# Rotary attention of a two-layer decoder: scores of two slots by 64-row strips, the maximum taken off by VectorE, one exponential to a slot

## The chip, the cores and the metric

The kernel runs on one core of one Trainium2 chip. The metric is the device time of one execution in microseconds (us). All data are float32. The engines are named as in the profile: PE is TensorE, DVE VectorE, ACT ScalarE, POOL GpSimd, SP SyncE.

## The reference, cut to what matters

A post-norm decoder of two layers works on 64 sequences of 128 tokens and 128 features. In each layer stand self attention, cross attention against a context of 77 positions, and a mixture of eight experts, each followed by a layer norm of `x + f(x)`. The change concerns the cross attention of the second layer alone, the "rotary" one:

```
q = rms_norm(heads(x @ Wq.T), q_norm_w)         # 16 heads of 8
k = rms_norm(heads(context @ Wk.T), k_norm_w)
v = heads(context @ Wv.T)
q, k = apply_rope(q, q_cos, q_sin), apply_rope(k, k_cos, k_sin)
attn = softmax(einsum('bhtd,bhsd->bhts', q, k) * 8 ** -0.5)
x = layernorm(x + einsum('bhts,bhsd->bhtd', attn, v) @ Wo.T)
```

## The kernel before

The program is six stages one behind the other: "taylor", "wide", "gelu", "causal", "rotary", "swiglu". Three of them ("wide", "causal", "rotary") are built by one function, `softmax_attention`, with `kind` choosing between variants. There is no scheduler: each engine has its instructions in the order in which the function `step` of that engine writes them, and engines meet at semaphores.

The work of the rotary stage is a pipeline over 32 pairs of sequences. A pair has `NU` = 8 **slots**; a slot is four heads (`HU`) of one sequence, so its scores are 128 queries by 4 x 77 keys. In one step an engine runs over the eight slots k = 0 to 7 and does at each what is due for pairs at different depths of the pipeline: `e` and `roots` (norm and rotation of a coming pair), `f` (turning queries and keys), `c` (scores of the current pair), `u` (its output), and behind these the layer norm and the choice of experts ("route") of older pairs.

For the current pair a slot goes like this. POOL makes `keys` of the slot (`make_keys`, L616): the transposed keys, repeated for four heads and multiplied by a mask that leaves each head its 8 rows of 128. PE multiplies the queries `qT` (128 rows, all 16 heads) with them into one of two PSUM banks `s_bank` (L982). DVE takes the negated maximum of each head (L1400). ACT does four exponentials, one to a head, out of the bank with that maximum as bias (L1116). PE transposes them (L991, two slots later), ACT copies them (L1103), and PE multiplies them with the values (L1014, three slots later); a column of ones among the values gives the softmax sum. The bank is free again when the exponentials have read it (`exps_done`).

Four uses share one further bank, `f_bank`, in this order within a pair: PE turns x and projects queries and keys of a coming pair (L728 at slot 0, L752/L753 at slot 1), and DVE reads the products with the rotation tables (L1452 at slot 2, L1454 and L1455 at slot 3); PE turns back the output sums of the first sequence (L911, slot 4) and DVE divides them (L1363, L1367, slot 4, waiting for `back_ps`); PE turns rotated queries and keys (L760, slot 5), for which it waits for that division (`norm_done`); the same division for the second sequence at slot 6, and the values (L756) at slot 7, which waits for it again. L925 turns the divided output, L930 projects it, L880 and L886 serve the choice of experts, and L1187 to L1195 are steps of an inverse root by Newton's method (12 to two pairs, one at slots 0 to 3 of every pair and at slots 4 to 7 of every second).

The causal stage has done since before what the change brings here: masks for eight heads (`heads8`), two matmuls of 64 rows each (L968), and DVE as the first reader of both banks (`add_slopes`, L1358).

Of the kernel before, what the change touches and what calls it, by code (L numbers as in the profile page):

```python
# [22 lines left out]
P = 128  # L23
# [370 lines left out]
def softmax_attention(chip, kind, n_seq, X, ctxT_dram, w, consts, route=None, fill=None, opening=None, later_loads=()):  # L394
# [5 lines left out]
    H = 16  # L400
# [19 lines left out]
    ES = 4 if kind == "causal" else 3 if late else SLOTS  # L420
    BS = 4
    KH = 8 if kind == "causal" else H
    with ExitStack() as ctx:
# [11 lines left out]
        keys = sb("keys", [P, 2, H, 2, NK] if kind == "wide" else [P, 2, KH, NK])  # L435
# [41 lines left out]
        if kind == "causal":  # L477
            biased = sb("biased", [P, BS, HU * NK])
            heads8 = sb("heads8", [P, KH])
            value_row = sb("value_row", [P, NC, P])  # L480
            q_bias = sb("q_bias", [P, 1])
# [43 lines left out]
        PREPARED = {"wide": 3, "causal": 4, "rotary": 10}[kind]  # L525
# [18 lines left out]
        POOL_KEYS = (0, 1)  # L544
# [3 lines left out]
        def first_head(j):  # L548

            return 8 * (j % 2) + 4 * (j // 2) if kind == "causal" else HU * j  # L550
# [57 lines left out]
        def make_keys(engine, pair, piece):  # L608

            engine.wait_ge(front_done, pair.count(FU, 1 if kind == "rotary" else 2))  # L610
            if pair.back(1).real:
                engine.wait_ge(s_ps, pair.back(1).count(NU, 2 * piece + 2 if kind == "causal" else piece + 1))
            b, j = divmod(piece, KH // HU)
            heads = slice(HU * j, HU * (j + 1))
            mask = heads8[:] if kind == "causal" else consts["heads16"]
            engine.tensor_tensor(keys[:, b, heads], kT[:, pair.c % 2, b, 0:NK].unsqueeze(1).to_broadcast([P, HU, NK]),  # L616
                                 mask[:, heads].unsqueeze(2).to_broadcast([P, HU, NK]),
                                 ALU.mult).then_inc(keys_done[piece % 2], 1)

        def keys_ahead(engine, f, c, k, pieces):  # L620

            pair, piece = (f, k - NU + KEYS_LEAD) if k >= NU - KEYS_LEAD else (c, k + KEYS_LEAD)
            if kind == "causal":
                if pair is not None and piece % 2 == 0:
                    make_keys(engine, pair, piece // 2)
            elif pair is not None and piece % 2 in pieces:
                make_keys(engine, pair, piece)

        @block.gpsimd
        def _(pool):  # L630
# [34 lines left out]
            def step(e, roots, f, c, u, n, r=None, *later):  # L665
                for k in range(NU):
                    if sending(later, k) is not None:
                        scatter(*sending(later, k))
                    if kind != "wide":
                        keys_ahead(pool, f, c, k, POOL_KEYS)  # L670
# [145 lines left out]
        def _(pe):  # L816
# [131 lines left out]
            def step(e, roots, f, c, u, mine=None, r=None, q=None, ranked=None, *later):  # L948
                for k in range(NU):
# [6 lines left out]
                    if c is not None:  # L956
# [3 lines left out]
                        if kind == "causal":  # L960
                            if k % 2 == 0:
                                pe.wait_ge(keys_done[k // 2 % 2], c.count(2, k // 4 + 1))
                                if before(c, k, 1) is not None:
                                    bc, bk = before(c, k, 1)
                                    pe.wait_ge(biased_done, bc.count(NU, bk + 1))
# [1143 lines left out]
```

## Time and profile before

| | |
|---|---|
| median of 3 runs | 3026.99 us (3024.47 to 3029.35) |
| profiled execution, its own time | 3017.08 us |
| its span | 3015.3 us |
| PE busy over the span | 2737.1 us (91%) |
| ACT | 2070.9 us (69%) |
| PEld (weight loads) | 1982.6 us (66%) |
| DVE | 1805.1 us (60%) |
| POOL | 1460.1 us (48%) |
| rotary scores on PE, 256 slots | 2061 us to 2600 us of the span |

### The profile page before, as it was taken

The page shows a single profiled execution, that of the slowest core. Times are in us where ns is not written, and L with a number is a line of the kernel's source. Part 1 is how long each engine was busy: PE and PEld are TensorE (multiplying, and loading weights), DVE is VectorE, ACT ScalarE, POOL GpSimd, SP SyncE. Part 2 cuts the span into 40 slices and gives each one's busy share as a digit, 9 for nine tenths or more (in the row PEclk, how much of TensorE's full clock was granted, in tenths as well). Part 3 has the DMA queues.
Part 4 walks back from the last instruction along what each step waited for, and adds up shares of the span by engine and source line. Part 5 has one row for each costly group of instructions (what it writes and reads, how often), then busy time and mean ns, then how long its engine had stood idle before and what let it go on. Part 6 is the DMA issues. An engine that isn't in the chain of part 4 may idle for free. (4 is left out here: it accounts for less than half of the span.)

```text
span 3015.3 us, 69304 instructions
## 1 busy us (share of the span) xinstructions
PE 2737.1 (91%) x21504; PEld 1982.6 (66%) x21504; DVE 1805.1 (60%) x5293; ACT 2070.9 (69%) x7235; POOL 1460.1 (48%) x1978
## 2 busy tenths in 40 slices
PE   8999999999999956998799999978999999699987
PEld 6666777777777746998355555546776666458874
DVE  6883344443444444554688888876677776444545
ACT  6766778777787743443699999976888888522224
POOL 3442224444444454555433333325678887724665
PEclk9999999999999987999899999998999999799998
DMA  9910030220400402221310000000000010001225
GB/s 264 338 47 15 19 116 16 80 78 20 129 27 20 135 30 72 73 70 57 115 56 10 9 10 8 10 22 10 13 27 28 29 31 17 29 26 56 80 79 185
DMA packets 179960, 185.08 MB, mean 61 GB/s; under 512 B 32844, under 2 KB 168537, under 8 KB 179216
## 3 DMA queue, kind: packets, MB, share of 16 engines
q1 hardware_dynamic: 162032, 145.14, 16.1%
q0 software_dynamic: 17280, 34.13, 3.4%
q8 instruction: 181, 2.97, 0.4%
q14 instruction: 179, 1.47, 0.2%
q10 hardware_dynamic: 288, 1.38, 0.2%
HBM read 58.34 MB, written 111.48 MB: 56 GB/s over the span
## 5 line engine op out<-in xcount | busy, mean ns | idle before, releaser
L678 POOL TENSOR_TENSOR wide_probs<-wide_exps,wide_inv_sum 128x308 f32<-128x308 f32 x256 | 179.3, 700 | 488.9 <-DVE wide_inv_sum L1409 486.0
L1400 DVE TENSOR_REDUCE wide_neg_max<-banks 128x4 f32<-128x308 f32 x256 | 122.5, 478 | 473.6 <-PE banks L982 448.9
L1116 ACT ACTIVATE causal_exps<-causal_biased,causal_neg_max 128x128 f32<-128x128 f32 x1024 | 325.8, 391 | 31.1 <-DVE causal_neg_max L1400 29.7
L1119 ACT ACTIVATE wide_exps<-banks,wide_neg_max 128x77 f32<-128x77 f32 x1024 | 315.8, 326 | 0.3 <-DVE wide_neg_max L1400 0.2
L658 POOL DMA_INDIRECT sorted_x<-send,place_i x240 | 244.9, 1020 | 96.0 <-issue 40.5
L1116 ACT ACTIVATE rotary_exps<-banks,rotary_neg_max 128x77 f32<-128x77 f32 x1024 | 252.0, 351 | 15.1 <-DVE rotary_neg_max L1400 13.7
L1103 ACT ACTIVATE wide_probsT<-banks 77x512 f32<-77x512 f32 x256 | 152.1, 594 | 153.6 <-PE banks L991 149.5
L1656 ACT ACTIVATE gelu_hidden<-banks,gelu_slot 128x256 f32<-128x256 f32 x284 | 116.7, 471 | 157.3 <-PE banks L1833 153.1
L1587 POOL DMA_INDIRECT results<-swiglu_tile_out,swiglu_dest_i x142 | 147.7, 1040 | 141.2 <-DVE swiglu_tile_out L1738 97.8
L1119 ACT ACTIVATION_READ_ACCUMULATOR wide_exps<-banks,wide_neg_max 128x1 f32 x1024 | 213.9, 209 | 0.0
L1587 POOL DMA_INDIRECT results<-gelu_tile_out,gelu_dest_i x142 | 140.8, 991 | 142.3 <-DVE gelu_tile_out L1743 119.0
L1358 DVE TENSOR_TENSOR causal_biased<-banks,regions 128x512 f32<-128x512 f32 x256 | 164.6, 685 | 72.3 <-PE banks L968 69.9
L1400 DVE TENSOR_REDUCE rotary_neg_max<-banks 128x4 f32<-128x308 f32 x256 | 121.5, 475 | 120.8 <-PE banks L982 116.4
L982 PE MATMUL banks<-wide_keys,wide_xT 128*128 128x308 f32 x512 | 191.8, 455 | 1.9 <-ACT wide_xT L769 1.6
L982 PE MATMUL banks<-rotary_keys,rotary_qT 128*128 128x308 f32 x512 | 189.0, 451 | 3.5 <-ACT rotary_exps L1116 3.4
L616 POOL TENSOR_TENSOR rotary_keys<-rotary_kT,rest 128x308 f32<-128x308 f32 x256 | 177.4, 708 | 20.0 <-ACT rotary_kT L803 16.5
L991 PEld LDWEIGHTS banks<-first,causal_exps 128*128 128x128 f32 x1024 | 108.9, 141 | 116.3 <-ACT causal_exps L1116 61.0
L1103 ACT ACTIVATE rotary_probsT<-banks 77x512 f32<-77x512 f32 x256 | 157.7, 616 | 34.7 <-PE banks L991 34.1
L735 PE MATMUL banks<-wide_ctxT,wide_product 128*128 128x154 f32 x1024 | 169.9, 299 | 3.3 <-ACT wide_product L1038 0.7
L1400 DVE TENSOR_REDUCE causal_neg_max<-causal_biased 128x4 f32<-128x512 f32 x256 | 169.6, 673 | 0.5 <-ACT causal_exps L1116 0.4
L991 PE MATMUL banks<-first,causal_exps 128*128 128x128 f32 x1024 | 166.1, 285 | 3.1 <-ACT causal_exps L1116 3.0
L1014 PE MATMUL banks<-wide_probsT,wide_values 77*64 77x128 f32 x2048 | 168.3, 285 | 0.1
(382 smaller groups left out, 7339.3 us busy)
## 6 DMA issues: line engine op xcount, KB each, us to landing
sorted_x<-blank SPq DMA_DIRECT2D x1, 34848.0 KB, 116.8
sorted_x<-blank SPq DMA_DIRECT2D x4, 8712.0 KB, 30.3
gelu_tile_in<-sorted_x SPq DMA_DIRECT2D x71, 132.0 KB
swiglu_tile_in<-sorted_x SPq DMA_DIRECT2D x71, 132.0 KB
gelu_back<-results SPq DMA_DIRECT2D x16, 512.0 KB, 7.7
swiglu_back<-results SPq DMA_DIRECT2D x16, 512.0 KB, 6.2
X<-in_x SPq DMA_DIRECT2D x8, 512.0 KB, 7.3
regions<-in_g_w SPq DMA_DIRECT2D x2, 2048.0 KB, 20.9
```

Source lines behind the costliest of these rows:

```text
L616: engine.tensor_tensor(keys[:, b, heads], kT[:, pair.c % 2, b, 0:NK].unsqueeze(1).to_broadcast([P, HU, NK]), mask[:, heads].unsqueeze(2).t ...
L658: pool.indirect_dma_start(route["sorted_x"], bass.IndirectOffsetOnAxis(ap=r_place_i[:, b % 2, which, n // 2:n // 2 + 1], axis=0), send[:, ...
L678: pool.tensor_tensor(probs[:, m % SLOTS], exps[:, m % SLOTS], inv_sum[:, m % SLOTS].unsqueeze(2).to_broadcast([P, HU, NK]), ALU.mult).then ...
L735: last = pe.matmul(f_bank[:, n * 2 * NK:(n + 1) * 2 * NK], product[:, first + n], ctxT[:, s4, :, 0:NK], start=True, stop=True)
L982: pe.matmul(s_bank[k % 2][:, 0:HU * NK], q, moving, start=True, stop=True).then_inc(s_ps, 1)
L991: last = pe.transpose(p_bank[n % 2][0:NK, h * P:(h + 1) * P], exps[:, (NU * pair.c + n) % ES, h] if late else probs[:, n % SLOTS, h], ident)
L1014: last = pe.matmul(o_bank[g % 2][row:row + STRIP, col:col + P], values[0:NK, pair.c % 2, b, first_head(j) + h], probsT[0:NK, n % 2, h * P: ...
L1103: act.activation(probsT[0:NK, n % 2], p_bank[n % 2][0:NK], ACT.Copy).then_inc(probsT_done, 1)
L1116: last = act.activation(exps[:, (NU * c.c + k) % ES, h], scores[:, h * NK:(h + 1) * NK], ACT.Exp, bias=neg_max[:, k % SLOTS, h:h + 1])
L1119: last = act.activation(exps[:, k % SLOTS, h], scores[:, h * NK:(h + 1) * NK], ACT.Exp, bias=neg_max[:, k % SLOTS, h:h + 1], accum_out=exp ...
L1400: dve.tensor_reduce(neg_max[:, k % SLOTS], scores.rearrange("p (h n) -> p h n", h=HU), AX.X, ALU.max, negate=True).then_inc(max_done, 1)
L1587: pool.indirect_dma_start(results, bass.IndirectOffsetOnAxis(ap=dest_i[:, t % YR, j:j + 1], axis=0), tile_out[:, t % YR, j], None, bounds_ ...
```

## The change

1. Keys are masked for eight heads instead of sixteen (`KH` = 8, `heads8`, one added DVE instruction in the stage's opening), so one POOL instruction serves two slots; queries and keys keep their 128 rows.
2. At every even slot PE does the scores of two slots as two matmuls of 64 rows: rows 0 to 63 (heads 0 to 7) into one bank, rows 64 to 127 (heads 8 to 15) into the other. The order of heads over slots changes with it (`first_head`).
3. At every even slot DVE takes the maxima of both slots (`find_top`) and then subtracts them, reading the banks and writing to SBUF (`take_top`, into `biased`). PE may use the banks again after that (`biased_done`), no longer after the exponentials.
4. ACT does one exponential of 308 columns to a slot, from `biased`, in place of four of 77. `exps` has four buffers instead of three.

```diff
-    ES = 4 if kind == "causal" else 3 if late else SLOTS
+    ES = 4 if late else SLOTS
-    KH = 8 if kind == "causal" else H
+    KH = 8 if late else H
...
-                engine.wait_ge(s_ps, pair.back(1).count(NU, 2 * piece + 2 if kind == "causal" else piece + 1))
+                engine.wait_ge(s_ps, pair.back(1).count(NU, 2 * piece + 2))
...
+                        if late and k % 2 == 0:
+                            pe.wait_ge(keys_done[k // 2 % 2], c.count(2, k // 4 + 1))
+                            if before(c, k, 1) is not None:
+                                bc, bk = before(c, k, 1)
+                                pe.wait_ge(biased_done, bc.count(NU, bk + 1))
+                            for n in range(2):
+                                rows = slice(64 * n, 64 * n + 64)
+                                pe.matmul(s_bank[n][:, 0:HU * NK], qT[rows, c.c % 2, b], keys[rows, b, HU * (j // 2):HU * (j // 2) + HU],
+                                          start=True, stop=True).then_inc(s_ps, 1)
...
-                        act.wait_ge(max_done, c.count(NU, k + 1))
-                        scores = biased[:, k % BS] if kind == "causal" else s_bank[k % 2]
+                        act.wait_ge(biased_done if kind == "rotary" else max_done, c.count(NU, k + 1))
+                        scores = biased[:, k % BS] if late else s_bank[k % 2]
...
+                        if kind == "rotary":
+                            last = act.activation(exps[:, (NU * c.c + k) % ES].rearrange("p h n -> p (h n)"), scores, ACT.Exp)
...
+                dve.tensor_tensor(heads8[:], consts["heads16"][:, 0:KH], consts["heads16"][:, KH:2 * KH], ALU.add).then_inc(prepared, 1)
...
+            def find_top(c, k):
+                dve.wait_ge(s_ps, c.count(NU, k + 1))
+                if before(c, k, SLOTS) is not None:
+                    bc, bk = before(c, k, SLOTS)
+                    dve.wait_ge(biased_done, bc.count(NU, bk + 1))
+                dve.tensor_reduce(neg_max[:, k % SLOTS], s_bank[k % 2][:, 0:HU * NK].rearrange("p (h n) -> p h n", h=HU), AX.X,
+                                  ALU.max).then_inc(max_done, 1)
+
+            def take_top(c, k):
+                dve.wait_ge(max_done, c.count(NU, k + 1))
+                if before(c, k, BS) is not None:
+                    bc, bk = before(c, k, BS)
+                    dve.wait_ge(exps_done, bc.count(NU, bk + 1))
+                dve.tensor_tensor(biased[:, k % BS].rearrange("p (h n) -> p h n", h=HU),
+                                  s_bank[k % 2][:, 0:HU * NK].rearrange("p (h n) -> p h n", h=HU),
+                                  neg_max[:, k % SLOTS].unsqueeze(2).to_broadcast([P, HU, NK]), ALU.subtract).then_inc(biased_done, 1)
...
+                    if c is not None and kind == "rotary" and k % 2 == 0:
+                        find_top(c, k)
+                        find_top(c, k + 1)
+                        take_top(c, k)
+                        take_top(c, k + 1)
```

How the order on two engines changes is seen in one pair. The first place is DVE in the fifth pair, from slot 2 to the first division at slot 4. Before:

```order
L1400 TENSOR_REDUCE rotary_neg_max<-banks 128x4
L1444 TENSOR_REDUCE rotary_qk_sum<-rotary_qk_sq 128x64
L1452 TENSOR_TENSOR rotary_turned<-banks,rotary_tables 128x512
L1193 SCALAR_TENSOR_TENSOR rotary_root_part<-rotary_root_part,rotary_qk_sum 128x128
L1400 TENSOR_REDUCE rotary_neg_max<-banks 128x4
L1454 TENSOR_TENSOR rotary_crossed<-banks,rotary_tables 128x64x4
L1455 TENSOR_TENSOR rotary_crossed<-banks,rotary_tables 128x64x4
L1195 SCALAR_TENSOR_TENSOR rotary_qk_rstd<-rotary_root_part,rotary_qk_rstd 128x128
L1400 TENSOR_REDUCE rotary_neg_max<-banks 128x4
L1363 RECIPROCAL rotary_inv_total<-banks 128x16
L1367 TENSOR_TENSOR rotary_o<-banks,rotary_inv_total 128x128
```

And changed, the same stretch (L1357 is `find_top`, L1365 `take_top`, L1372 and L1376 the division):

```order
L1357 TENSOR_REDUCE rotary_neg_max<-banks 128x4 x2
L1365 TENSOR_TENSOR rotary_biased<-banks,rotary_neg_max 128x308 x2
L1458 TENSOR_REDUCE rotary_qk_sum<-rotary_qk_sq 128x64
L1466 TENSOR_TENSOR rotary_turned<-banks,rotary_tables 128x512
L1185 SCALAR_TENSOR_TENSOR rotary_root_part<-rotary_root_part,rotary_qk_sum 128x128
L1468 TENSOR_TENSOR rotary_crossed<-banks,rotary_tables 128x64x4
L1469 TENSOR_TENSOR rotary_crossed<-banks,rotary_tables 128x64x4
L1187 SCALAR_TENSOR_TENSOR rotary_qk_rstd<-rotary_root_part,rotary_qk_rstd 128x128
L1357 TENSOR_REDUCE rotary_neg_max<-banks 128x4 x2
L1365 TENSOR_TENSOR rotary_biased<-banks,rotary_neg_max 128x308 x2
L1372 RECIPROCAL rotary_inv_total<-banks 128x16
L1376 TENSOR_TENSOR rotary_o<-banks,rotary_inv_total 128x128
```

One reduction stood ahead of the division; four instructions do now, and the same four stand in one block at slots 0, 2 and 6.

The second place is PE in the same pair, slots 4 and 5 and the score of slot 6. Before:

```order
L982 MATMUL banks<-rotary_keys,rotary_qT 128x308
L991 MATMUL banks<-first,rotary_exps 77x128 x4
L911 MATMUL banks<-first,rotary_sums 128x128 x4
L1014 MATMUL banks<-rotary_probsT,rotary_values 32x128 x4
L982 MATMUL banks<-rotary_keys,rotary_qT 128x308
L991 MATMUL banks<-first,rotary_exps 77x128 x4
L760 MATMUL banks<-first,rotary_scaled 128x128 x4
L1014 MATMUL banks<-rotary_probsT,rotary_values 32x128 x4
L982 MATMUL banks<-rotary_keys,rotary_qT 128x308
```

Changed (L963 is the score, L979 the transposes, L907 the turning back, L756 the turning of queries and keys, L1002 the product with the values):

```order
L963 MATMUL banks<-rotary_keys,rotary_qT 128x308 x2
L979 MATMUL banks<-first,rotary_exps 77x128 x4
L907 MATMUL banks<-first,rotary_sums 128x128 x4
L1002 MATMUL banks<-rotary_probsT,rotary_values 32x128 x4
L979 MATMUL banks<-first,rotary_exps 77x128 x4
L756 MATMUL banks<-first,rotary_scaled 128x128 x4
L1002 MATMUL banks<-rotary_probsT,rotary_values 32x128 x4
L963 MATMUL banks<-rotary_keys,rotary_qT 128x308 x2
```

The score of slot 5 has moved up to slot 4; the score of slots 6 and 7 stands behind the turning of queries and keys, as that of slot 6 did.

## Rows read from the trace of the kernel before

**Rows 1.** Stretches of the rotary stage: busy time of each engine, clock, DMA
```profile
core 0: us, PE busy (x) PEld busy (x) DVE busy (x) ACT busy (x) POOL busy (x), PEclk, DMA share, GB/s
2061.00:2600.00 539.00, 513.10 (x4719) 370.73 (x4718) 377.16 (x1058) 476.46 (x1742) 409.93 (x523) 1.00 0.08 23
2120.70:2136.80 16.10, 16.10 (x152) 11.78 (x151) 8.60 (x26) 14.53 (x53) 10.26 (x15) 1.00 0.05 14
2306.60:2325.80 19.20, 17.75 (x166) 12.60 (x165) 17.95 (x47) 16.76 (x62) 15.67 (x20) 1.00 0.10 27
2325.80:2342.60 16.80, 15.68 (x145) 11.62 (x144) 10.95 (x37) 14.04 (x53) 13.44 (x18) 1.00 0.10 31
2342.60:2361.10 18.50, 17.27 (x165) 12.32 (x163) 14.55 (x32) 16.22 (x61) 15.38 (x19) 1.00 0.09 27
2361.10:2376.70 15.60, 15.34 (x143) 11.33 (x140) 10.86 (x33) 14.39 (x55) 13.44 (x18) 1.00 0.12 32
```

**Rows 2.** Groups of instructions by line and shape, 2061 to 2600 us
```profile
L1116 ACT ACTIVATE rotary_exps<-banks,rotary_neg_max 128x77 f32<-128x77 f32 x1024 | 252.0, 351 | 15.1 <-DVE rotary_neg_max L1400 13.7 <-PE banks L991 1.1
L616 POOL TENSOR_TENSOR rotary_keys<-rotary_kT,rest 128x308 f32<-128x308 f32 x253 | 175.3, 708 | 19.4 <-ACT rotary_kT L803 15.9
L1193 DVE SCALAR_TENSOR_TENSOR rotary_root_part<-rotary_root_part,rotary_qk_sum 128x128 f32<-128x128 f32 x43 | 36.3, 844 | 0.0
L1452 DVE TENSOR_TENSOR rotary_turned<-banks,rotary_tables 128x512 f32<-128x512 f32 x27 | 18.4, 680 | 0.0
L1454 DVE TENSOR_TENSOR rotary_crossed<-banks,rotary_tables 128x256 f32<-128x256 f32 x27 | 11.1, 413 | 0.0
```

**Rows 3.** Waits, 2061 to 2600 us: us in total, times, longest
```profile
DVE rotary_neg_max L1400 <- PE banks L982: 115.0, 130, 2.2
PE banks L760 <- DVE rotary_o L1367: 8.0, 9, 1.1
```

**Rows 4.** Timeline of the fifth pair: start, us, instruction, idle before it
```profile
2119.99 0.69 PE L982 MATMUL banks<-rotary_keys,rotary_qT 128*128 128x308 f32 x2
2120.51 0.60 PE L991 MATMUL banks<-first,rotary_exps 128*77 128x128 f32 x4
...
2124.73 0.68 PE L982 MATMUL banks<-rotary_keys,rotary_qT 128*128 128x308 f32 x2
...
2125.85 0.68 DVE L1444 TENSOR_REDUCE rotary_qk_sum<-rotary_qk_sq 128x64 f32<-128x512 f32 x1
...
2127.24 0.47 DVE L1400 TENSOR_REDUCE rotary_neg_max<-banks 128x4 f32<-128x308 f32 x1
...
2128.29 0.28 DVE L1195 SCALAR_TENSOR_TENSOR rotary_qk_rstd<-rotary_root_part,rotary_qk_rstd 128x128 f32<-128x128 f32 x1
...
2131.11 0.60 PE L760 MATMUL banks<-first,rotary_scaled 128*128 128x128 f32 x4
...
2131.99 0.79 PE L982 MATMUL banks<-rotary_keys,rotary_qT 128*128 128x308 f32 x2
...
2133.94 0.33 PE L925 MATMUL banks<-first,rotary_o 128*128 128x128 f32 x1
...
2134.11 0.69 PE L982 MATMUL banks<-rotary_keys,rotary_qT 128*128 128x308 f32 x2
```

**Rows 5.** Timeline of the causal stage, one even slot
```profile
1724.14 1.13 PE L968 MATMUL banks<-causal_keys,causal_qT 64*128 64x512 f32 x4
1725.20 0.66 PE L991 MATMUL banks<-first,causal_exps 128*128 128x128 f32 x4
1725.30 1.29 DVE L1358 TENSOR_TENSOR causal_biased<-banks,regions 128x512 f32<-128x512 f32 x2 [0.32 <-PE banks L968]
1726.51 0.68 DVE L1400 TENSOR_REDUCE causal_neg_max<-causal_biased 128x4 f32<-128x512 f32 x1
```

**Rows 6.** Timeline of the 18th pair of the rotary stage, slots 4 and 5
```profile
2351.52 2.17 DVE L1193 SCALAR_TENSOR_TENSOR rotary_root_part<-rotary_root_part,rotary_qk_sum 128x128 f32<-128x128 f32 x1
...
2352.29 1.25 POOL L650 TENSOR_TENSOR rotary_rotated<-rotary_turned,rotary_crossed 128x512 f32<-128x512 f32 x1
...
2353.61 0.25 DVE L1363 RECIPROCAL rotary_inv_total<-banks 128x16 f32<-128x16 f32 x1
...
2354.44 0.63 PE L760 MATMUL banks<-first,rotary_scaled 128*128 128x128 f32 x4 [0.97 <-DVE rotary_o L1367]
```

More of the change, by code:

```diff
@@ L542, in softmax_attention @@
         TURNS = 3
-        POOL_KEYS = (0, 1)
         MLAG = 1
@@ L548, in first_head @@
         def first_head(j):
-            return 8 * (j % 2) + 4 * (j // 2) if kind == "causal" else HU * j
+            return 8 * (j % 2) + 4 * (j // 2) if late else HU * j
         def lagged(c, u, k, lag):
@@ L611, in make_keys, with keys_ahead @@
             if pair.back(1).real:
-                engine.wait_ge(s_ps, pair.back(1).count(NU, 2 * piece + 2 if kind == "causal" else piece + 1))
+                engine.wait_ge(s_ps, pair.back(1).count(NU, 2 * piece + 2))
             b, j = divmod(piece, KH // HU)
             heads = slice(HU * j, HU * (j + 1))
-            mask = heads8[:] if kind == "causal" else consts["heads16"]
             engine.tensor_tensor(keys[:, b, heads], kT[:, pair.c % 2, b, 0:NK].unsqueeze(1).to_broadcast([P, HU, NK]),
-                                 mask[:, heads].unsqueeze(2).to_broadcast([P, HU, NK]),
+                                 heads8[:, heads].unsqueeze(2).to_broadcast([P, HU, NK]),
                                  ALU.mult).then_inc(keys_done[piece % 2], 1)
[L620 to L627, printed above, removed]
+        def keys_ahead(engine, f, c, k):
+            pair, slot = (f, k - NU + KEYS_LEAD) if k >= NU - KEYS_LEAD else (c, k + KEYS_LEAD)
+            if pair is not None and slot % 2 == 0:
+                make_keys(engine, pair, slot // 2)
         @block.gpsimd
@@ L959, in step @@
                             pe.wait_ge(front_done, c.count(FU, 1 if kind == "rotary" else FU))
[L960 to L965, printed above, removed]
-                                for n in range(2):
-                                    rows = slice(64 * n, 64 * n + 64)
-                                    pe.matmul(s_bank[n][:, 0:HU * NK], qT[rows, c.c % 2, b], keys[rows, b, HU * (j // 2):HU * (j // 2) + HU],
-                                              start=True, stop=True).then_inc(s_ps, 1)
-                        else:
-                            if kind == "rotary":
-                                pe.wait_ge(keys_done[k % 2], c.count(NU // 2, k // 2 + 1))
+                        if late and k % 2 == 0:
[7 more added lines that the diff above has]
+                                          start=True, stop=True).then_inc(s_ps, 1)
+                        if not late:
                             if before(c, k, 2) is not None:
```

39 lines of the change are left out of this document (18 added, 21 removed).

## Prediction

> **What bounds the kernel now.** The change touches one of six stages, so I first cut the span by stretches. Between 2061 and 2600 us, 539 us in all, PE is busy 513.10 us, ACT 476.46, POOL 409.93 and DVE 377.16, at a granted clock of 1.00 [rows 1]. The stage isn't uniform. The fifth pair of sequences takes 16.10 us and PE is busy through all of it: PE bounds it, ACT (14.53) is close behind, and DVE (8.60) has half its time free. From about the twelfth pair on, when the choice of experts fills DVE and POOL too, the pairs come in a pattern of four: 19.20, 16.80, 18.50 and 15.60 us, 70.1 us together. In the first of these DVE is busy 17.95 of 19.20 us. So there are some 11 pairs bound by PE, some 17 in which DVE and PE take turns, and the last ones.
>
> The waits say who is late where: DVE's reductions wait 115.0 us for scores, which is DVE's spare time; PE waits for the division (L760 for `rotary_o`) 9 times, 8.0 us in all [rows 3]. That second row is small now, and it is the one to watch.
>
> **What the change removes, adds and moves.**
>
> *POOL* has 128 instructions fewer of 708 ns [rows 2]: 91 us of 410. They lie beside other work. They matter only where DVE cannot start an instruction while POOL is at work: L1193 takes 2.17 us while POOL works on L650 [rows 6], and 0.28 us is what its sister L1195 takes undisturbed [rows 4]. Over the stage L1193 has a mean of 844 ns x 43 [rows 2], so its stretching alone is (0.84 - 0.28) x 43 = 24 us. I count a part of it back below, as 1 us in a heavy pair.
>
> *ACT* has one exponential of 308 columns for four of 77 (252.0 us busy over 256 slots, 0.98 us to a slot [rows 2]). The trace has no such instruction; the bounds are one of 77 columns (0.35 us) and all four (0.98 us), and by ACT's other shapes I take 0.45 us. That takes off 0.53 us x 256 = 136 us of ACT work. ACT isn't the last to arrive in the bounding waits, so I count nothing for it; what hides it is PE's own row of work, and if PE ran out of it ACT would be at some 340 us, far from a bound.
>
> *PE.* Two scores now hold PE 0.52 us each (2119.99 to 2120.51 [rows 4]). The causal stage shows two strips of 64 rows and 512 columns holding it 1.06 us together (1724.14 to 1725.20 [rows 5]); for 308 columns that is 0.64 us. Bounds: 0.52 (the two quite beside each other) and 1.04 (one after the other). I take 0.64, since it is the same form. PE saves 0.4 us to two slots, 1.6 us to a pair, 51 us in all, if nothing else held it.
>
> The Trainium skill (TensorEngine Tiling, Theoretical Speedup) gives up to twofold for a contraction of 64 rows or fewer; the causal strips show less. By that rule the two strips would take 0.52 us, each of the three legs below that begins with a score would be 0.12 us shorter, and the sum would end near 3027 us. The same page (Key Properties) says that a change of tiling mode drains the engine, which would speak against the change; no row of the causal stage shows a cost of it beyond the 1.06 us.
>
> *DVE* gets 256 subtractions of 308 columns out of PSUM. Tensor-tensor instructions with a PSUM operand take 680 ns for 512 columns and 413 for 256 [rows 2]; in between, 308 columns give 0.47 us, as the reduction does (0.47 [rows 4]). From start to start the 512-column form is 0.61 us apart (two in 1.29 us, 0.68 each [rows 5]); less 204 columns, that is 0.39 us. So DVE gets 256 x 0.39 = 100 us more and would be near 470 of 539 us. The bounds are 0.32 us (308 columns at the slope alone) and 0.47.
>
> *What moves* decides. PE, DVE and the shared bank `f_bank` now form a ring. Two scores can only be overwritten after four DVE instructions, and the division, for which L760 and L756 (slots 5 and 7) wait, stands behind those four instead of behind one. I follow the ring through a pair without expert choice:
>
> 1. Score of slot 0 to score of slot 2: PE's own row. Now 4.74 us (2119.99 to 2124.73 [rows 4]); less two scores of 0.52, plus 0.64: 4.34.
> 2. Score of slot 2 to the first maximum: 1.16 us for a hold of 1.06 in the causal stage [rows 5], so 0.64 + 0.10 = 0.74. Four DVE instructions at 0.39: 1.57. Then L1444, L1452, L1193, L1454, L1455 and L1195: 2128.29 - 2125.85 = 2.44 with one reduction among them (0.39) and L1195 behind (0.20): 2.25 [rows 4]. PE is ready with the score of slot 4 before that. The next four instructions: 1.57. From the reciprocal to L760: 2353.61 to 2354.44, 0.83 us [rows 6]. L760 and L1014 until the score of slot 6: 0.88 us (2131.11 to 2131.99 [rows 4]). Together 7.84.
> 3. Score of slot 6 to the next pair: 0.74 + 1.57 + 0.83 + 0.88, and 0.17 for L925 (2133.94 to 2134.11 [rows 4]): 4.19.
>
> That is 16.37 us, and 0.4 us more in every second pair, where a root step stands ahead of each division: 16.6 us on average against 16.1 now, though PE alone would need only 14.5. For the first 11 pairs, of which the first few are shorter, the pipeline not being full, I count +6 us.
>
> For the pattern of four: in the heavy pair DVE gets 8 x 0.39 = 3.1 us on top of 17.95, gets back 1 us of stretching, and has still to wait a little at slot 6: 20.3 for 19.2. The second follows the ring with some instructions of the expert choice on it: 16.9 for 16.8. The third has 14.55 + 3.1 us of DVE work, its stretched L1193 partly sheltered: 18.0 for 18.5. The fourth follows the ring: 16.6 for 15.6. Together 71.8 for 70.1, +1.7 us to four pairs, +7 us for 17. The last four pairs, with no coming pair behind them, gain some 2 us. The sum is +11 us, on the profiled execution 3017 + 11 = 3028, and on the median of the runs 3027 + 11 = **3038 us**. The median of runs lies 10 us above the profiled execution, and I take the difference as the same for both kernels.
>
> **Rivals.**
>
> *Faster: the ring doesn't close, and engine work decides.* For: PE saves 51 us, ACT 136, POOL 91, all three close to full today, and the stretched DVE instructions (2.17 us for 0.28 [rows 6]) shrink with the keys; ring legs of mine are sums of start-to-start distances whose lags may partly overlap. Against: L760 waits for the division today where DVE is late by only one instruction more [rows 3, 6]. If it holds, a light pair takes 15.3 us (PE's 14.5 and small gaps) and four later pairs 66 us (DVE 54.3 + 12.5 - 4, at 95%): -9 us and -17 us, 3001 us. It decides once the ring is below 16.1 us, 0.5 us less than I find. Chance 0.28.
>
> *No difference:* the ring is about as long as today's pair, as with strips quite beside each other. About 3027 us. Chance 0.2.
>
> *Slower by much: DVE becomes the bound and stays late.* The subtraction costs 0.47 us start to start, stretching stays as it is since POOL's other instructions hold DVE instead, and the four later pairs take 77 us: 17/4 x 7 = 30 us, and 1.2 us to each of 11 light pairs, 13 us: 3070 us. For: DVE is at 17.95 of 19.20 us in the heavy pair [rows 1]. Against: in three pairs of four it has 4 to 5 us free. Chance 0.12. The forecast case itself (3033 to 3055 us) has 0.4.
>
> That the strips run one after the other (1.04 us) is part of the last rival: it would add 0.4 us to each of three legs and to PE's row.
>
> **How the numbers follow.** The bound of what a measurement of this kernel tells from no change is 0.2%, 6 us. Slower: the forecast case 0.4 and the large loss 0.12, less some of the forecast near +6: 0.5. Within: 0.22. Faster: 0.28. The range leaves out the far tenth at each end: 3003 to 3066 us, taking in most of the faster rival and the loss up to a DVE that is steadily late.
>
> **What would show it.** In the rotary stage: L963 pairs held 0.64 us; `take_top` near 0.47 us; the exponential near 0.45 us; ACT near 340 us, POOL near 320, DVE near 470; PE's waits for the division (L756 and L752 for `rotary_o`) up from 8.0 us to 20 us or more, at every pair, and a light pair of 16.4 to 17 us with gaps on PE where there are none today. I am wrong if light pairs come out under 16 us, if L756 doesn't wait, or if another stage moves by more than 2 us, since no instruction of theirs changes.

## The result and the profile after

| | before | changed |
|---|---|---|
| median of 4 runs each, same chip | 3027.63 us (3024.47 to 3029.35) | 3058.14 us (3056.93 to 3060.05) |
| ratio | | 1.0103, interval 1.0085 to 1.012 |
| profiled execution, own time | 3017.08 us | 3059.29 us |
| its span, mean granted clock | 3015.3 us | 3057.5 us, 0.957 |

The changed kernel is 1.0% slower: +30.5 us between the medians, where +11 was forecast. Two things in that sum are to be kept apart. The profiled execution of before lay 10 us below its median, that of the change within 2 us of its own, so the two traces differ by 42.2 us. Of these, 35.2 us lie between the first score of the rotary stage and the first score of its last pair, 2.3 ahead of that and some 4.7 behind. The traces say where the loss sits; the medians say how large it is.

These are the stretches of the changed kernel, for [rows 1]: the stage, the fifth pair and the sixth, and then four pairs of the later pattern (the 20th to the 23rd). Each pair here runs from its first score to the first score of the next one.

```profile
core 0: us, PE busy (x) PEld busy (x) DVE busy (x) ACT busy (x) POOL busy (x), PEclk, DMA share, GB/s
2061.00:2620.00 559.00, 501.29 (x4580) 327.40 (x4578) 422.52 (x1274) 359.39 (x944) 315.50 (x388) 0.94 0.07 21
2126.70:2143.40 16.70, 15.47 (x151) 10.20 (x150) 11.21 (x34) 11.18 (x29) 7.47 (x10) 1.00 0.05 15
2143.40:2161.00 17.60, 15.57 (x151) 10.22 (x150) 12.23 (x38) 11.32 (x29) 7.52 (x10) 1.00 0.05 13
2402.80:2424.40 21.60, 18.52 (x151) 11.91 (x150) 18.26 (x53) 12.02 (x33) 13.82 (x17) 0.84 0.09 27
2424.40:2445.20 20.80, 19.22 (x159) 12.96 (x158) 14.55 (x48) 12.04 (x33) 11.17 (x14) 0.84 0.07 21
2445.20:2462.50 17.30, 15.49 (x151) 10.18 (x150) 13.19 (x39) 12.11 (x33) 10.61 (x14) 1.00 0.10 30
2462.50:2479.40 16.90, 15.66 (x151) 10.21 (x150) 13.04 (x39) 12.02 (x34) 11.25 (x14) 1.00 0.10 29
```

PE, ACT and POOL have all lost work, ACT 117 us and POOL 94, and no engine fills the stage: PE is busy 501 of 559 us, where it was busy 513 of 539. In the fifth pair, which PE filled before, it now has 1.2 us of gaps. The last number that matters is the clock: 0.94 over the stage, and 0.84 in two of the four later pairs, where [rows 1] shows 1.00 everywhere.

The groups by line and shape, 2055 to 2640 us, for [rows 2]:

```profile
L1103 ACT ACTIVATE rotary_exps<-rotary_biased 128x308 f32<-128x308 f32 x256 | 116.6, 455 | 35.5 <-DVE rotary_biased L1365 29.9
L1357 DVE TENSOR_REDUCE rotary_neg_max<-banks 128x4 f32<-128x308 f32 x256 | 110.5, 473 | 118.5 <-PE banks L963 117.4
L1365 DVE TENSOR_TENSOR rotary_biased<-banks,rotary_neg_max 128x308 f32<-128x308 f32 x256 | 109.3, 469 | 0.0
L615 POOL TENSOR_TENSOR rotary_keys<-rotary_kT,rotary_heads 128x308 f32<-128x308 f32 x128 | 89.6, 703 | 59.1 <-ACT rotary_kT L799 57.7
L1185 DVE SCALAR_TENSOR_TENSOR rotary_root_part<-rotary_root_part,rotary_qk_sum 128x128 f32<-128x128 f32 x45 | 21.5, 477 | 0.3
```

The exponential (455 ns for 450 forecast) and the subtraction (469 for 470) cost what was forecast. The waits, 2061 to 2620 us, for [rows 3]:

```profile
DVE rotary_neg_max L1357 <- PE banks L963: 116.3, 83, 3.3
PE banks L756 <- DVE rotary_o L1376: 26.6, 22, 2.4
PE banks L752 <- DVE rotary_o L1376: 8.5, 15, 0.9
PE banks L891 <- DVE rotary_r_logits L1206: 7.9, 6, 1.4
```

PE now waits 35.1 us for the division, 37 times, where it waited 8.0 us 9 times. DVE meanwhile waits 116.3 us for scores, as much as before: it isn't short of time, it and PE wait for each other in turns. This is the fifth pair from its slot 4 on (PE's rows, then DVE's), for [rows 4]:

```profile
2134.68 0.79 PE L963 MATMUL banks<-rotary_keys,rotary_qT 64*128 64x308 f32 x4
2135.40 0.66 PE L979 MATMUL banks<-first,rotary_exps 128*77 128x128 f32 x4
...
2136.79 0.66 PE L979 MATMUL banks<-first,rotary_exps 128*77 128x128 f32 x4
2138.26 0.63 PE L756 MATMUL banks<-first,rotary_scaled 128*128 128x128 f32 x4 [0.81 <-DVE rotary_o L1376]
...
2139.17 0.79 PE L963 MATMUL banks<-rotary_keys,rotary_qT 64*128 64x308 f32 x4
...
2135.88 0.86 DVE L1357 TENSOR_REDUCE rotary_neg_max<-banks 128x4 f32<-128x308 f32 x2
2136.65 0.85 DVE L1365 TENSOR_TENSOR rotary_biased<-banks,rotary_neg_max 128x308 f32<-128x308 f32 x2
2137.43 0.25 DVE L1372 RECIPROCAL rotary_inv_total<-banks 128x16 f32<-128x16 f32 x1
```

Two maxima, two subtractions, the reciprocal, and then L756, for which PE has stood 0.81 us; only behind it comes the score of slot 6. That is the ring of the prediction. The same place in the 20th pair shows what the prediction had not seen:

```profile
2412.92 1.07 DVE L1218 TENSOR_TENSOR rotary_r_equal<-rotary_r_choice,rotary_r_key_top 128x64 f32<-128x64 f32 x1
2414.03 0.86 DVE L1357 TENSOR_REDUCE rotary_neg_max<-banks 128x4 f32<-128x308 f32 x2
...
2413.57 0.66 PE L979 MATMUL banks<-first,rotary_exps 128*77 128x128 f32 x4
2416.61 1.09 PE L756 MATMUL banks<-first,rotary_scaled 128*128 128x128 f32 x4 [2.37 <-DVE rotary_o L1376]
...
2418.21 1.40 PE L963 MATMUL banks<-rotary_keys,rotary_qT 64*128 64x308 f32 x4
2419.54 1.13 PE L979 MATMUL banks<-first,rotary_exps 128*77 128x128 f32 x4
```

PE stands 2.37 us, and what it does next takes about twice its time: the strips 1.40 for 0.79, the transposes 1.13 for 0.66. The granted clock is at the lower of its two levels, half of full, from 2416.0 for 6.8 us. The changed kernel has ten such stretches inside the stage, of 3.4 or 6.8 us, 54.6 us together; before had none between 2062.6 and 2605.3. Each begins inside an idle stretch of PE or at most 1.4 us behind its end. The five stretches of 2.37 us all brought one, four of the five of 1.37 us did (for L891, which waits for the router's logits; the one in the 17th pair did not), and one came behind 0.81 us. Of the other idle stretches of 0.80 us or more, 23 of up to 1.03 us, none did.

### The profile page after: what moved, and what is told of

Same layout as the page of the kernel before. It is cut to its first block and busy times, and to the rows that moved or that the text cites. A ratio compares the mean times of both kernels' runs of the same rounds, so it can differ in the third digit from the quotient of the medians.

```text
span 3057.5 us, 68684 instructions
## 1 busy us (share of the span) xinstructions
PE 2739.5 (90%) x21504; PEld 1946.2 (64%) x21504; DVE 1861.4 (61%) x5550; ACT 1962.7 (64%) x6467; POOL 1372.1 (45%) x1850
## 5 line engine op out<-in xcount | busy, mean ns | idle before, releaser
L1091 ACT ACTIVATE rotary_probsT<-banks 77x512 f32<-77x512 f32 x256 | 150.9, 589 | 116.7 <-PE banks L979 115.1
L979 PEld LDWEIGHTS banks<-first,causal_exps 128*128 128x128 f32 x1024 | 109.2, 141 | 116.2 <-ACT causal_exps L1107 61.0
L1357 DVE TENSOR_REDUCE rotary_neg_max<-banks 128x4 f32<-128x308 f32 x256 | 110.5, 473 | 118.5 <-PE banks L963 117.4
L979 PE MATMUL banks<-first,rotary_exps 128*77 128x128 f32 x1024 | 172.9, 294 | 0.0
L979 PE MATMUL banks<-first,causal_exps 128*128 128x128 f32 x1024 | 166.6, 285 | 3.1 <-ACT causal_exps L1107 3.0
L1002 PE MATMUL banks<-wide_probsT,wide_values 77*64 77x128 f32 x2048 | 168.3, 285 | 0.1
L979 PEld LDWEIGHTS banks<-first,rotary_exps 128*77 128x77 f32 x1024 | 121.2, 155 | 68.7 <-ACT rotary_exps L1103 35.4
L979 PEld LDWEIGHTS banks<-first,wide_probs 128*77 128x77 f32 x1024 | 130.0, 146 | 48.5 <-issue 0.2
## 6 DMA issues: line engine op xcount, KB each, us to landing
regions<-in_g_w SPq DMA_DIRECT2D x2, 2048.0 KB, 20.2
```

What stands on the lines that cost most here:

```text
L979: last = pe.transpose(p_bank[n % 2][0:NK, h * P:(h + 1) * P], exps[:, (NU * pair.c + n) % ES, h] if late else probs[:, n % SLOTS, h], ident)
L1002: last = pe.matmul(o_bank[g % 2][row:row + STRIP, col:col + P], values[0:NK, pair.c % 2, b, first_head(j) + h], probsT[0:NK, n % 2, h * P: ...
L1091: act.activation(probsT[0:NK, n % 2], p_bank[n % 2][0:NK], ACT.Copy).then_inc(probsT_done, 1)
```

## The experiments

The theory after the result: the ring costs the time, by the place of the division behind four DVE instructions. Rival A: the DVE work itself costs it, wherever it stands. Rival B: the clock drops cost it and the ring only sets them off. Rival C: the strips or the subtraction are worth less than assumed, each by itself. "Light" are the fifth and sixth pair; "heavy" are the first and second of each pattern of four, from the 12th pair on, and the eighth and ninth.

### The division after two instructions instead of four

```diff
                         find_top(c, k)
                         find_top(c, k + 1)
+                        if u is not None and k in (4, 6):
+                            divide(u, (k - 4) // 2)
                         take_top(c, k)
                         take_top(c, k + 1)
```

(`divide` is left out at its old place.)

> The changed kernel with one thing moved: at slots 4 and 6 of the rotary stage DVE does the division between the two maxima and the two subtractions, so two DVE instructions stand ahead of it instead of four; the same work otherwise. Ring theory (PE and DVE wait for each other through the shared bank): the legs with a division lose about 1 us and 0.6 us, a light pair falls from 16.8 to 17.6 us to 15.3 to 15.8 us, PE's wait for the division falls from 35 us to under 10 us, the clock keeps its full level, 3058 us becomes 3005 to 3025 us. Rival, DVE is simply too full: the same number of DVE instructions, so the pairs and the time stay within 8 us of 3058 us.

3016.18 us (3015.37 to 3020.79) against 3026.41; ratio 0.9966, interval 0.9954 to 0.9977. No work is removed, four instructions change places, and 42 us go. The fifth pair takes 15.58 us. Its slot 4, DVE's rows and then PE's:

```profile
2132.33 0.85 DVE L1357 TENSOR_REDUCE rotary_neg_max<-banks 128x4 f32<-128x308 f32 x2
2133.10 0.24 DVE L1372 RECIPROCAL rotary_inv_total<-banks 128x16 f32<-128x16 f32 x1
...
2133.59 0.85 DVE L1365 TENSOR_TENSOR rotary_biased<-banks,rotary_neg_max 128x308 f32<-128x308 f32 x2
...
2133.93 0.63 PE L756 MATMUL banks<-first,rotary_scaled 128*128 128x128 f32 x4
```

L756 has no wait any more in this pair; over the stage it waits 7.0 us in 5 places, up to 1.4 us, in heavy pairs. Half-clock stretches in the stage fall to 5, 23.9 us, where the expectation had a full clock throughout. The place of the division costs the time, then; whether by the waits themselves or by the clock drops behind them (rival B) this run can't tell.

### Doses: three ahead, five ahead, and the same work elsewhere

```diff
                         take_top(c, k)
+                        if k in (4, 6):
+                            find_again(k, k // 2 - 2)
                         take_top(c, k + 1)
```

`find_again` is one more reduction of a bank, into a spare buffer that nobody reads. In the first kernel (five ahead) it stands as shown; in the second both repetitions stand at slot 0, where no division follows; in the third there is none, and the division stands between the two `take_top` (three ahead).

> The changed kernel with one more reduction of 308 columns on DVE at slots 4 and 6 (its result unused), so five instructions stand ahead of each division: 64 instructions of about 0.39 us start to start, 25 us of DVE work. Ring theory: every light pair grows by 2 x 0.39 = 0.8 us (16.8 to 17.5, 17.6 to 18.3), 3058 us becomes 3080 to 3095 us. Rival, the total of DVE work decides: the same time as with the two reductions at slot 0.

> The changed kernel with the same 64 reductions, but both at slot 0, where DVE afterwards waits 1.3 us for the score of slot 2 in a light pair. Ring theory: light pairs stay at 16.8 and 17.6 us, the whole at 3054 to 3066 us. Rival, total of DVE work: as long as with the reductions at slots 4 and 6, 3080 us or more.

> The changed kernel with the division between the first and the second subtraction, three instructions ahead of it. Ring theory: the even light pair loses 0.8 us, 16.76 to 16.0 us, between four ahead (16.76) and two ahead (15.58, where PE's own row is the floor); 3025 to 3040 us. Rival, a threshold rather than a slope: it stays at 16.76 us or falls to 15.58 us at once.

All against 3021.56 us on their chip. The leg is the time from the score of slot 4 to that of slot 6 in the fifth pair, by the traces' score rows:

| DVE instructions ahead of the division | leg, us | light pairs, us | median, us | ratio |
|---|---|---|---|---|
| 2 (the kernel above) | 3.71 | 15.58 / 15.58 | 3016.18 | 0.9966 |
| 3 | 4.09 | 15.99 / 15.92 | 3023.34 (3017.13 to 3033.61) | 1.0013 (0.9998 to 1.0027) |
| 4 (the change) | 4.48 | 16.76 / 17.57 | 3058.14 | 1.0103 |
| 4, two more at slot 0 | 4.48 | 16.75 / 17.47 | 3053.85 (3051.53 to 3054.43) | 1.0111 (1.0094 to 1.0128) |
| 5 | 4.87 | 17.53 / 17.95 | 3087.42 (3086.61 to 3092.68) | 1.0225 (1.0208 to 1.0243) |

The leg grows by 0.39 us with each instruction, the start-to-start price of the prediction. The fifth pair has two such waits and grows by 0.8 us from three to four and from four to five; from two to three it grows by 0.4, since the leg from slot 6 on is then PE's own row (3.86 and 3.88 us). The time with two at slot 0 and that with three are just under what was expected (3054 to 3066, and 3025 to 3040), the fifth pair is as expected each time. The sixth isn't with five ahead: 17.95 for 18.3. Two reductions more cost 1.1% ahead of the divisions and nothing that can be told (1.0111 for 1.0103) at slot 0: rival A falls. The steps in the time are uneven, though. From two to three it is some 0.5%, from three to four 0.9%, from four to five 1.2%. Half-clock time in the stage is 23.9, 23.9, 54.6 and 64.8 us in the four traces: waits and half-clock time grow together from four on.

The ten executions of the kernel with three ahead show what the clock adds, since nothing else was changed between them. They lie on a line: the four with a mean granted clock of 0.960 or 0.961 took 3017.1 to 3019.3 us, the four at 0.952 to 0.955 took 3028.0 to 3033.6. From the fastest to the slowest it is 16.5 us for 0.009 of clock, which is some 54 us more at half clock: 0.3 us for each. So the step from two to three is 0.2% at like clock, and the rest of it is clock. That the time follows the clock doesn't say that all of it is caused by it; longer waits could bring both.

### PE kept busy through the waits

```diff
-                        for h in range(HU):
+                        for h in list(range(HU)) * (3 if kind == "rotary" and k in (5, 7) else 1):
                             last = pe.transpose(p_bank[n % 2][0:NK, h * P:(h + 1) * P],
```

The transposes of slots 5 and 7, just ahead of the two waits, are done three times over. The second kernel does this at slot 5 alone.

> The changed kernel with PE's four transposes of slots 5 and 7 done three times each (same result, 8 transposes more, 0.9 us, ahead of the place where PE waits for the division). Theory that the drops of PE's granted clock in the heavy pairs (55 us at half clock within the stage) come from PE's idle stretch at that wait: the drops vanish, heavy pairs lose 2 to 3 us, light pairs stay within 0.3 us, 3058 us becomes 3035 to 3045 us although PE has 28 us of work more. Rival, the drops cost nothing or have another cause: they stay, and the time is the same or up to 25 us longer.

> The changed kernel with PE's four transposes of slot 5 alone done three times (0.9 us more ahead of the wait for the division, nothing at slot 7, whose repeats made every pair 0.45 us longer before). Theory that the drops of PE's clock follow from its idle stretch at slot 5 and cost 2.7 us of a heavy pair: even light pairs stay at 16.76 us, most drops are gone, 3058 us becomes 3040 to 3052 us. Rival, the drops cost nothing of the time: within 5 us of 3058 us whatever the clock does.

The first: 3063.19 us (3060.58 to 3066.89) against 3026.41, ratio 1.0124 (1.0107 to 1.0141). The second: 3053.98 us (3049.34 to 3056.16) against 3026.19, ratio 1.0090 (1.0073 to 1.0107). Their windows of the stage, the first kernel and then the second:

```profile
2061.00:2620.00 559.00, 531.42 (x5073) 371.07 (x5069) 425.72 (x1273) 357.31 (x943) 315.45 (x386) 0.98 0.07 21
```

```profile
2061.00:2620.00 559.00, 519.23 (x4866) 351.27 (x4865) 428.01 (x1286) 365.49 (x954) 317.36 (x390) 0.97 0.07 21
```

The clock comes back (0.98 and 0.97 for 0.94; half-clock time 13.7 and 23.9 us for 54.6), the time doesn't. In the first kernel the repetitions at slot 7 cost 0.45 us a pair themselves (the last leg is 4.72 for 4.27), which hides a gain. In the second they cost nothing in light pairs (16.76 and 17.48), and more than half the half-clock time goes for some 4 us, within the two intervals. The theory's ranges were missed by both; the second time lies in the rival's.

That doesn't make the drops cheap, since the repetitions are not free in every pair. The 17th pair has no drop in either trace and takes 18.02 us in the changed kernel, 19.04 in the second one here; the 29th takes 17.81 and 21.00. The price of a drop is read inside one trace, from pairs of the same place in the pattern with the same wait. In the changed kernel the 17th pair has the wait of 1.37 us and no drop, and takes 18.02 us; the 13th, 21st and 25th have that wait and a drop of 6.8 us, and take 20.72 to 20.74:

```profile
2350.40:2368.40 18.00, 16.20 (x157) 10.89 (x156) 14.49 (x45) 12.03 (x33) 9.73 (x12) 1.00 0.09 25
```

Against the row 2424.40:2445.20 above, DVE has the same work (14.49 and 14.55 us), and PE is busy 3.0 us longer for its own: 2.7 us of pair for 6.8 us at half clock, 0.4 us for each. In the fastest kernel below, the 12th and 24th pair wait 1.48 us without a drop and take 17.65 us; the 16th and 20th, with the same wait and a drop of 3.4 us, take 19.2. In the second kernel here the same comparison gives 0.7 us (19.40 and 20.10) for 3.4. At 0.3 to 0.4 us for each, the 54.6 us of the changed kernel are an estimated 16 to 22 us of the 35 that the pairs lost in the trace. By this estimate rival B holds for about half the loss: the ring's waits set the drops off, and the drops cost about as much again as the waits. It doesn't hold for the whole: the first seven pairs lose 7.1 us and have no drop.

### Strips without the subtraction, and the subtraction without strips

The strips alone: four exponentials of 77 columns to a slot read the bank with their bias, as before, and the banks come free behind them.

```diff
-                                pe.wait_ge(biased_done, bc.count(NU, bk + 1))
+                                pe.wait_ge(exps_done if kind == "rotary" else biased_done, bc.count(NU, bk + 1))
```

The subtraction alone, from the kernel before: a score of 128 rows to each slot, keys masked for sixteen heads, two buffers of `biased` and three of `exps` (the whole change has four of each; the waits in this run's trace name neither).

```diff
+                    if c is not None and kind == "rotary":
+                        find_top(c, k)
+                        take_top(c, k)
```

> Only the matmuls by 64-row strips and the keys for eight heads; four exponentials to a slot out of the bank as before, no subtraction, the banks free after the exponentials of both slots. Ring theory: one DVE instruction ahead of the division, but the banks of a pair of slots come free only after eight exponentials (2 us) that start after the maxima, PE at the score of the next two slots waits for ACT; 3030 to 3060 us, the wait now for rotary_exps. Rival, only the subtraction costs: PE keeps its saving of 1.3 us to a pair and the time is 3000 to 3020 us.

> Only the subtraction on DVE and the single exponential (from the kernel before; one matmul of 128 rows to a slot, keys for 16 heads, two buffers for the subtracted scores since memory holds no more). Two DVE instructions per slot ahead of the division instead of one. Ring theory: light pairs stay near PE's 16.1 us, heavy pairs get 3 us of DVE work longer, in all 3030 to 3050 us. Rival, the block of four (not the added work) costs everything: within 6 us of 3027 us.

Strips alone: 3213.29 us (3210.74 to 3216.07), ratio 1.0619 (1.0602 to 1.0637), six times the loss of the whole change. Its wait, 2061 to 2780 us, and its window:

```profile
PE banks L963 <- ACT rotary_exps L1107: 134.6, 121, 2.2
```

```profile
2061.00:2780.00 719.00, 563.76 (x4689) 371.89 (x4690) 342.32 (x1054) 486.31 (x1729) 325.34 (x397) 0.87 0.06 17
```

With both banks filled at once, nothing fills the time in which eight exponentials empty them; the mechanism was as expected, its size wasn't; 180.9 us at half clock stand in the stage too. The subtraction is what makes strips bearable at all.

Subtraction alone: 3071.91 us (3068.7 to 3074.18), ratio 1.0146 (1.0129 to 1.0163), also dearer than expected. Its windows of the fifth pair and of the stage:

```profile
2125.10:2141.60 16.50, 16.32 (x151) 11.81 (x151) 12.97 (x35) 11.46 (x30) 10.25 (x15) 1.00 0.05 14
...
2061.00:2640.00 579.00, 531.08 (x4644) 378.97 (x4644) 485.52 (x1295) 364.74 (x959) 406.05 (x518) 0.96 0.07 21
```

A light pair loses 0.4 us against before, the first and second pair of each pattern 2.3 to 5.4 (20.4 to 23.4 us each), and 44.4 us are at half clock. DVE is busy 485 us of 579, where the whole change has it at 422 of 559 with much the same instructions, and POOL 406 us for 316. That POOL holds DVE up more is the reading that fits; it wasn't tried by itself. So neither half gains alone, and the whole is better than either: rival C in the form "one part is good, the other bad" falls.

### The logits too, and the choice steps behind

The first kernel adds to the early division that `take_logits` (L1206), for which PE's L891 waits, stands at slot 4 ahead of both `take_top`. The second adds to this that at even slots the steps of the expert choice stand behind `take_top`.

```diff
+                        if r is not None and k == 4:
+                            take_logits(r)
                         if u is not None and k in (4, 6):
                             divide(u, (k - 4) // 2)
                         take_top(c, k)
                         take_top(c, k + 1)
+                        choice()
```

(the last line in the second kernel only)

> The run with the division between maxima and subtractions, and in addition the copy of the router's logits moved from slot 5 to slot 4 between maxima and division: PE waits 8.7 us in 7 places for that copy (1.4 us at most) before it ranks. If that wait is on the path, 3016 us becomes 3005 to 3011 us; if something else is late there, it stays within 3 us.

> The run with the division and the logits moved ahead, and at even slots also the steps of the expert choice behind the two subtractions instead of ahead of the maxima (one of them takes 1.07 us behind POOL at slot 4 of a heavy pair, and the division stands behind it). Ring theory: light pairs stay at 15.6 us, heavy pairs lose 1 to 2 us, 3007 us becomes 2998 to 3004 us. Rival, DVE is full in heavy pairs, so the order of its own work doesn't matter: within 3 us of 3007 us.

The first: 3006.67 us (3002.97 to 3008.57) against 3021.56, ratio 0.9950 (0.9933 to 0.9967). It is the fastest of all and beats both kernels. The wait of L891 goes from 8.7 us to 0.8, and these are its 17th pair, the 16th and the fifth (the 16th is the first of a pattern of four, the 17th the second):

```profile
2325.60:2342.00 16.40, 15.91 (x159) 10.91 (x158) 14.45 (x44) 11.57 (x33) 10.67 (x14) 1.00 0.10 31
2306.40:2325.60 19.20, 17.08 (x151) 11.03 (x150) 17.10 (x54) 11.90 (x34) 13.28 (x17) 0.91 0.09 27
2121.30:2136.90 15.60, 15.29 (x150) 10.21 (x150) 11.50 (x35) 10.78 (x29) 7.47 (x11) 1.00 0.06 16
```

The second pair of the pattern takes 16.35 us in the 17th and 21st, where it was 17.6 to 17.9 with the early division alone: the rank matmuls no longer wait. Its counterparts, the 13th and 25th, take 22.41 and 17.93; both have an idle PE of 1.11 us ahead of L876 instead, and the 13th a drop of 10.2 us.

The second kernel: 3024.92 us (3022.39 to 3045.62) against 3026.19, ratio 1.0004 (0.9989 to 1.0019), a miss. The first pair of the pattern falls to 16.6 us as hoped, but the next takes 20.2 to 22.2. The 17th pair shows why, DVE's rows and then PE's:

```profile
2321.36 1.77 DVE L1224 TENSOR_TENSOR rotary_r_second<-rotary_r_ranked,rotary_r_rank_top 128x64 f32<-128x64 f32 x1
...
2325.52 0.85 DVE L1357 TENSOR_REDUCE rotary_neg_max<-banks 128x4 f32<-128x308 f32 x2
...
2328.18 0.41 PE L876 MATMUL banks<-first,X 128*128 128x128 f32 x2 [1.80 <-issue]
```

The steps put behind slot 6's `take_top` stand ahead of the next pair's first maximum, and are stretched there (L1224 1.77 us for 0.22). The maximum comes 3.4 us behind the strips' start at 2322.09, PE runs dry for 1.80 us, and the clock falls (0.85 in that pair, which takes 22.18 us). The 21st and 25th pair have the same 1.80 us without a drop and take 20.17, 3.8 us more than the 17th pair above: the late maximum costs by itself.

## Why the prediction was right in sign and short in size

**Cost of single instructions:** right within 2%: exponential 0.455 for 0.45 us, subtraction 0.469 for 0.47, start to start 0.39 for 0.39. POOL is at 316 us for "near 320". ACT, at 359 of 559, is above "near 340" and DVE, at 423, below "near 470"; the DVE forecast added 100 us to 377 and took nothing off for stretching, while L1185's mean (L1193 before) fell from 844 to 477 ns, 16 us by itself.

**Two strips hold PE 0.64 us:** wrong; they hold it 0.72 (2134.68 to 2135.40). The rule of the Trainium skill (TensorEngine Tiling, Theoretical Speedup), up to twofold, would have them at 0.52, what one score of 128 rows takes. Two scores took 1.04 one after the other, so the gain measured here is 1.04 / 0.72 = 1.4-fold.

**PE alone would need 14.5 us:** wrong, and the larger part of the light pairs' miss. Even with its waits gone, in the fastest kernel, PE is busy 15.29 of 15.60 us. The prediction took off the scores and left all else. But the transposes behind the strips hold PE 0.50 us (2135.40 to 2135.90), where they held it 0.43 before (from 2120.51 [rows 4] to the row below), and those of slots 2 and 3 hold it 0.60 (2131.97 to 2132.57 and 2132.92 to 2133.52 in the changed kernel), where the same slots took 0.53 before.

```profile
2120.94 0.38 PE L728 MATMUL banks<-first,rotary_xin 128*128 128x128 f32 x2
...
2132.57 0.42 PE L1002 MATMUL banks<-rotary_probsT,rotary_values 77*32 77x128 f32 x8
```

**The ring's three legs:** right in mechanism and nearly in size for the fifth pair: 4.58, 7.91 and 4.27 us for 4.34, 7.84 and 4.19, together 16.76 for 16.37. The first leg carries the miss, by the two items above. "0.4 us more in every second pair" was 0.8: the root step L1183 ahead of slot 6's division takes 0.66 us in the sixth pair, at 2158.53, while POOL works on L706. The first eleven pairs lost 14.6 us for +6: 7.1 in the first seven, and 7.6 in the next four, where the first choice steps and two of the half-clock stretches already lie.

**The pattern of four:** the step that fell short most: the pairs lost 24 us more than forecast in the traces, 14 of them here. Forecast was +1.7 us to a pattern; over the four full ones it is +5.4 each on average, 21.4 us in all for +7; the last four pairs gained 0.9 for 2. To see in which pair, the base has to be cut at the same marks. The stretches of [rows 1] (19.20, 16.80, 18.50 and 15.60 us) begin up to 2 us behind the first scores; from score to score the 16th to 19th pair of the kernel before are

```profile
2305.80:2323.82 18.02, 16.57 (x152) 11.79 (x151) 16.20 (x46) 15.58 (x58) 14.65 (x20) 1.00 0.10 29
2323.82:2341.86 18.04, 16.92 (x158) 12.49 (x158) 12.90 (x39) 15.28 (x58) 14.51 (x19) 1.00 0.10 29
2341.86:2359.47 17.61, 16.38 (x151) 11.80 (x151) 12.92 (x31) 15.33 (x58) 14.59 (x19) 1.00 0.10 28
2359.47:2375.93 16.46, 16.20 (x152) 11.82 (x152) 12.32 (x33) 15.25 (x58) 14.21 (x18) 1.00 0.11 30
```

with the same sum of 70.1. The forecast changes were +1.1, +0.1, -0.5 and +1.0 us; the 20th to 23rd pair (21.60, 20.73, 17.35 and 16.94) show +3.6, +2.7, -0.3 and +0.5. The third and fourth are as forecast or better. The second is as forecast where the clock stays full (18.02 in the 17th pair; 18.29 in the 13th of the kernel with two more at slot 0, also without a drop) and 2.7 us longer where it drops; by these pairs its whole miss is the clock. For the first, every instance has a drop; taken off at 0.4 us for each us, an estimated 18.7 to 19.8 us is left, +0.7 to +1.8. The step that failed is therefore the clock: the prediction read 1.00 for the whole stage [rows 1] and carried it over, although it itself put waits on PE, and seven of the sixteen pairs came to run in part at half clock. "A little wait at slot 6" of the first pair was a 2.37 us one at slot 4. The wait of L891 for the logits (up to 1.4 us), which stand behind the four instructions too, was not in the forecast either; it sets off the second pair's drops, and without it and without a drop the second pair falls from 17.6 to 16.35 us.

**Rivals:** "faster, the ring doesn't close" is contradicted by L756's wait in light pairs, yet it names the number that counts: once the division is moved the light pair takes 15.6 us (15.3 was its figure) and the kernel 3007 to 3016 us (3001). "DVE becomes the bound and stays late" is contradicted by DVE's 116.3 us of waiting for scores; its time, 3070, was closer than the forecast's 3038 for another reason. The forecast case was put at 3033 to 3055 us, and the range went on to 3066 to take in a part of that rival; that the measured 3058 lies inside is in part luck. The 10 us between the profiled execution and the median, taken as the same for both kernels, were 10 before and -1 after.

**Left open:** the exact price of the clock drops, for which the twin pairs give from 0.2 to 0.5 us for each us at half clock, and why the same wait brings a drop in one pair and not in another; and the 7 us by which the two traces differ outside the pairs, against "no more than 2 us", which one profile of each can't tell from the spread between executions.

## What to carry to other kernels

When instructions are added to an in-order engine, ask who waits for what stands behind them. Here each one from the fourth on cost 0.39 us at each of two waits in a light pair, and the same work elsewhere cost nothing that can be told; moving the division ahead of two of them turned +1.0% into -0.3%, and the logits with it into -0.5%. And when a change puts waits of 1.4 to 2.4 us on a TensorE whose longest was 1.07 us, the durations read at full clock no longer hold for what follows: by the estimate above that was about half of the loss here.

## What the hardware showed that was not expected

- **The clock falls inside a stage that stays busy.** PE at 501 of 559 us was granted half clock ten times, in or just behind single idle stretches of 0.8 to 2.4 us. The same idle stretch brings a drop in one pair and none in another: 2.37 us in five of five, 1.37 us in four of five (the changed kernel), 1.48 us in two of five (the fastest). A drop of 6.8 us made the pair 2.7 us longer.
- **The same transposes hold PE 0.43 to 0.60 us**, by their neighbours: 0.43 between two full-height matmuls; 0.50 after the strips; 0.53 after a full-height matmul where the products with the values come next; 0.60 where these come next and the strips or other such products came before. Why isn't shown.
- **The held-up DVE instructions have all their operands in SBUF**: L1224 1.77 us for 0.22, L1218 1.07 for 0.22, L1183 0.66 for 0.28, each while POOL was at work on a tensor instruction in the trace. The 256 subtractions out of PSUM took 460 to 476 ns, the shortest and the longest of them. Where a step of the first kind stands ahead of something that PE waits for, its stretching lands on PE, as L1218 in the 20th pair and L1224 in the last experiment.
